# Two graph attention layers in one kernel: the order of chunk 0, the place of layer two's operands, and the order of the mask checks

## The chip, the cores and the metric

One core of a Trainium2 chip. The metric is the device time of one execution in microseconds; the median of several runs is compared.

## What is computed

Two graph attention layers over 4096 nodes with 128 features and a dense 0/1 adjacency matrix `adj` (int32, 4096 x 4096), each followed by a residual and a layer norm:

```python
# layer one, 4 heads of 32
Wh = (h @ W).reshape(N, H, D)
e = leaky_relu(s_src[:, None, :] + s_dst[None, :, :], 0.2)
attention = softmax(where(adj > 0, e, -9e15), axis=1)
x = layernorm(x + elu(einsum('ijh,jhd->ihd', attention, Wh)))
# layer two, hyperbolic maps at the origin
x_tan = logmap0(x)
e = leaky_relu(x_tan @ a[:D] + (x_tan @ a[D:]).T, 0.2)
attention = softmax(where(adj > 0, e, -9e15), axis=1)
x = layernorm(x + proj(expmap0(attention @ x_tan)))
```

## The kernel before

Leaky ReLU has two slopes, so exp(leaky(s_i + d_j)) is a product of a row factor and a column factor on either side of s_i + d_j = 0. The kernel therefore never forms the attention matrix. For each pair it makes two 0/1 masks in fp8 ("above" and "below": edge and sign of the score) and multiplies them on TensorE with column factors times values. These values are kept in three bf16 parts (high, middle, rest) side by side, so that their sum has float32's precision: `moving`, W0 = 198 columns for a head of layer one (2 sides x 3 parts x 33), and 2 x 3 x 129 = 774 columns for a tile of 128 nodes in layer two, 387 for one side.

**Layer one** goes over NC = 4 chunks of 1024 rows. A chunk has U = 32 units: 4 heads times 8 units of JU = 4 column tiles (`u = 8 * head + g`). The masks of a unit are made by ScalarE (`act_unit`, L545, four Sign activations of 1024 elements) or by VectorE (`dve_compare`, L558), as the table `ON_ACT` says, and put together with the edges by VectorE (`dve_unit`: L577 behind ScalarE, L581 behind the comparison, and L587 for the units that need a second mask, by the table `DIRECT`). TensorE then does 64 matmuls (`pe_unit`, L610). `ring` has six slots for units, so ScalarE and VectorE can be up to six units ahead. Behind the second unit of the next head VectorE evacuates a head (`take_head`, L626 to L635); TensorE needs these banks for the next head. The matrix arrives by DMA, is turned on TensorE (`turn_quarter` and `turn_group`) and copied to `masks` by ScalarE (`take_quarter`, L448, and `take_group`, L468). Chunk 0 comes in four quarters, and its values are prepared head by head: `weigh_values` and `take_high` and `take_middle` on VectorE (L480 to L492), `round_part` on ScalarE (L498), in turns. `elu_exp`, `close_piece` and `hidden_sum` close a chunk during the next one.

**Layer two** goes over NR = 8 runs of 512 rows. A run has RT = 4 row tiles and NG = 4 groups of GT = 8 column tiles; 256 matmuls of 387 columns (L969 in runs 0 and 1, group by group; L982 in runs 2 to 7, row tile by row tile). Its masks are kept in DRAM by layer one (`masks_kept`) and loaded per run. ScalarE writes the signs of a group (`signs`, L692, eight activations), VectorE makes both masks of it (`split_group`, L705 and L708). When TensorE has done a row tile of a run, VectorE evacuates it (`evacuate_run`, L716, eight reductions for a run), which frees its two banks for the next run, and then `finish_run` closes the run: L725 to L728, and the closing of L290 to L327 with three activations of ScalarE in between (L336), the last of which is asked for by L322. The operands of layer two are made in four groups of eight tiles: `weigh_group` (L653, L654), `take_high1` (L664), `take_middle1` (L670) on VectorE and `round_part1` (L677) on ScalarE. They need the scores of layer two: roots (L1044), logarithms (L1047) and exponentials (`late_exp`, L763 to L767) on ScalarE between `roots_ask`, `logs_ask`, `gains` and `late_weights` (L1126 to L1131) on VectorE, once for tiles 0 to 23 (EARLY) inside the last chunk, and once for the last eight tiles behind it. Before the change only group 0 is made inside the last chunk.

**Checks.** The kept masks must be 0 or 1. VectorE ORs all of them together in 32 parts (`check_part`, L735), each loaded by GpSimd's queue (L892) in one of three buffers. `raise_flag` looks at the result at the end of run 6.

The order of work is written out by hand: every engine has a loop over c, u (and e in layer two), and `if u == ...` places the extra work behind a unit. Waits are on counting semaphores; an engine works strictly in its program's order. `dve_unit(dve, c, u)` also starts the comparison of unit u + 1, ahead of u's own operations.

## Time and profile before

| | us |
|---|---|
| median of 3 runs | 972.5 (971.72 to 977.3) |
| the profiled execution | 975.74 |
| its span, first to last instruction | 974.0 |
| TensorE busy (matmuls) | 856.1 |
| VectorE busy | 769.9 |
| ScalarE busy | 674.0 |
| GpSimd busy | 43.3 |
| mean granted clock of TensorE | 0.956 |

The profile is of one execution. Its timelines give the start and length of instructions on each engine, the idle time before them and what ended it. Matmuls are pipelined, so the distance between starts is what one costs; the length given for one is longer. "PE" is TensorE's matmuls, "DVE" VectorE, "ACT" ScalarE, "SPq" and "POOLq" the queues from which DMAs are issued. The chunks of layer one end near 183, 305, 428 and 559 us of the span, the runs of layer two lie between 560 and 951.

### The profile page before, as it was taken

How to read it: one execution, taken by the hardware profiler on the slowest of the kernel's cores; microseconds unless marked ns; L12 is line 12 of the kernel's file. 1: busy time of each engine (PE TensorE's matmuls, PEld its weight loads, DVE VectorE, ACT ScalarE, POOL GpSimd, SP SyncE). 2: the span in 40 equal slices, each digit the busy share in tenths (PEclk: the TensorE clock that was granted, in tenths of full speed). 3: DMA queues.
4: the chain of work that ended last, by engine and by line, in shares of the span. 5: the costliest groups of instructions: out<-in, count | busy, mean ns of one | idle time of the engine just before them, and what ended most of it. 6: DMA issues, size and time to landing. Idle time of an engine off the chain costs nothing.

```text
span 974.0 us, 24352 instructions
## 1 busy us (share of the span) xinstructions
PE 856.1 (88%) x10868; PEld 698.2 (72%) x10868; DVE 769.9 (79%) x1312; ACT 674.0 (69%) x789; POOL 43.3 (4%) x80
## 2 busy tenths in 40 slices
PE   8468999989999899999998994899999999879890
PEld 6467999989999899999997952455555555445450
DVE  3857898899988999889976897868565858575865
ACT  3868988888999879999889864873845444426101
POOL 2200000000000000000000000000000010100000
PEclk9879999999999999999999997899999899989995
DMA  8988278704568036040301040202032424241320
GB/s 143 172 83 207 61 72 95 223 23 48 68 75 229 24 38 75 25 196 24 104 9 24 2 152 1 87 23 98 11 109 71 168 81 158 95 159 43 104 87 13
DMA packets 41906, 84.66 MB, mean 87 GB/s; under 512 B 6211, under 2 KB 31173, under 8 KB 41157
## 3 DMA queue, kind: packets, MB, share of 16 engines
q0 software_dynamic: 12416, 33.56, 23.7%
q1 hardware_dynamic: 29380, 49.50, 14.4%
q8 instruction: 86, 1.41, 0.6%
q14 instruction: 24, 0.19, 0.1%
HBM read 112.27 MB, written 21.12 MB: 137 GB/s over the span
## 4 chain that ended last, share of the span: by engine, by line
PE 51%; DVE 27%; ACT 14%; issue 4%; DMA 3%; SPq 0%; DVEq 0%; ACTq 0%
PE bank L610 32%; PE bank L982 9%; ACT masks L692 9%; PE bank L969 6%; DVE ring L558 4%; DVE ring L577 3%; DMA moving<-masks_kept 3%; ACT ring L545 2%; PE bank L461 2%; ACT masks L448 2%; DVE ring L735 1%; DVE ring L587 1%; DVE ring L716 1%; DVE ring L581 1%; ACT moving L498 1%
## 5 line engine op out<-in xcount | busy, mean ns | idle before, releaser
L610 PE MATMUL bank<-moving,ring 128*128 128x99 bf16 (+1 forms) x6400 | 460.5, 220 | 11.6 <-DVE ring L587 7.9
L610 PEld LDWEIGHTS bank<-moving,ring 128*128 128x128 fp8e4 x6400 | 390.3, 98 | 15.3 <-DVE ring L587 8.8
L545 ACT ACTIVATE ring<-s_rows,scores 128x1024 fp8e4<-128x1024 f32 x356 | 377.5, 1142 | 15.6 <-PE bank L610 14.2
L610 PE MATMUL bank<-moving,masks 128*128 128x99 bf16 x1792 | 241.5, 209 | 28.5 <-DVE ring L577 17.2
L610 PEld LDWEIGHTS bank<-moving,masks 128*128 128x128 fp8e4 x1792 | 175.9, 98 | 30.9 <-DVE ring L577 18.1
L982 PE MATMUL bank<-moving,masks 128*128 128x387 bf16 x1152 | 195.9, 328 | 0.0
L982 PEld LDWEIGHTS bank<-moving,masks 128*128 128x128 fp8e4 x1152 | 112.9, 98 | 79.4 <-issue 0.5
L692 ACT ACTIVATE masks<-s_rows,adj_tiles 128x512 fp8e4<-128x512 f32 x256 | 157.8, 709 | 0.1
L336 ACT ACTIVATE ring<-ring 128x4 f32<-128x4 f32 x24 | 4.9, 205 | 190.1 <-DVE ring L292 157.2
L577 DVE SCALAR_TENSOR_TENSOR ring<-ring,masks 128x1024 int32<-128x1024 int32 x89 | 108.4, 1219 | 4.7 <-ACT ring L545 4.7
L587 DVE TENSOR_TENSOR ring<-masks,ring 128x1024 int32<-128x1024 int32 x72 | 88.2, 1225 | 26.3 <-PE bank L610 24.6
L558 DVE TENSOR_SCALAR ring<-s_rows,neg_d 128x1024 uint8<-128x1024 f32 x156 | 107.0, 751 | 0.0
L982 PE MATMUL bank<-adj_tiles,masks 128*128 128x387 bf16 x384 | 73.5, 347 | 20.5 <-DVE ring L716 20.5
L705 DVE SCALAR_TENSOR_TENSOR masks<-masks 128x1024 int32<-128x1024 int32 x32 | 39.2, 1224 | 62.7 <-ACT masks L692 62.6
L969 PE MATMUL bank<-moving,masks 128*128 128x387 bf16 x384 | 65.9, 332 | 20.5 <-DVE masks L708 20.5
L982 PEld LDWEIGHTS bank<-adj_tiles,masks 128*128 128x128 fp8e4 x384 | 39.0, 102 | 51.4 <-DVE ring L716 22.0
L969 PEld LDWEIGHTS bank<-moving,masks 128*128 128x128 fp8e4 x384 | 37.8, 99 | 48.5 <-DVE masks L708 21.7
L468 ACT ACTIVATE masks<-bank 128x1024 uint16<-128x1024 uint16 x48 | 48.5, 1016 | 19.6 <-PE bank L461 18.7
L735 DVE TENSOR_TENSOR ring<-ring,moving 128x1024 int32<-128x1024 int32 x32 | 39.2, 1224 | 19.4 <-DMA moving<-masks_kept 18.2
L581 DVE TENSOR_TENSOR ring<-ring,masks 128x1024 int32<-128x1024 int32 x39 | 47.5, 1218 | 0.0
L626 DVE TENSOR_REDUCE evac<-bank 128x132 f32<-128x396 f32 x64 | 32.8, 562 | 12.7 <-PE bank L610 12.3
L892 POOL DMA_DIRECT2D moving<-masks_kept x32 | 17.0, 531 | 536.3 <-DVE ring L735 353.9
(179 smaller groups left out, 604.5 us busy)
## 6 DMA issues: line engine op xcount, KB each, us to landing
masks_kept<-masks SPq DMA_DIRECT2D x4, 4096.0 KB, 18.3
masks<-masks_kept SPq DMA_DIRECT2D x8, 2048.0 KB, 12.0
moving<-masks_kept POOLq DMA_DIRECT2D x32, 512.0 KB, 5.0
adj_tiles<-in_adj_dram POOLq DMA_DIRECT2D x24, 512.0 KB, 8.3
s_rows<-score_rows SPq DMA_DIRECT2D x14, 512.0 KB, 5.8
adj_tiles<-in_adj_dram POOLq DMA_DIRECT2D x16, 256.0 KB, 15.3
feat<-in_x_dram SPq DMA_DIRECT2D x4, 512.0 KB, 5.7
values_kept<-masks SPq DMA_DIRECT2D x1, 2048.0 KB, 14.3
```

Of the source, the lines that this page charges most:

```text
L468: act.activation(dst[:, j:j + GQ, t * P:(t + 1) * P], turn_bank[q % 4][:, :].bitcast(U16).rearrange("p (j i) -> p j i", i=P), ACT.Copy, bi ...
L545: last = act.activation(j_tile(below, k), s_rows[:, h % 2, :], ACT.Sign, bias=scores[:, g * JU + k, h:h + 1], saturate=False)
L558: last = dve.tensor_scalar(j_tile(below, k), s_rows[:, h % 2, :], neg_d[:, h, j:j + 1], float(TWO), ALU.is_lt, ALU.mult)
L577: dve.scalar_tensor_tensor(out=below, in0=below, scalar=1, in1=m, op0=ALU.logical_shift_right, op1=ALU.bitwise_and).then_inc(done, 1)
L581: dve.tensor_tensor(below, below, m, ALU.bitwise_and).then_inc(done, 1)
L587: dve.tensor_tensor(above_slot(c, u).bitcast(I32), m, below, ALU.bitwise_xor).then_inc(unit_ready, 1)
L610: last = pe.matmul(bank[b][:, at + lo:at + hi], mask, moving[:, j, h, lo:hi], start=first, stop=(j == T - 1), skip_group_check=True)
L692: last = act.activation(j_tile1(sides_of_run[y][1], j), s_rows1[:, y, :], ACT.Sign, bias=d1[:, j:j + 1], saturate=False)
L705: dve.scalar_tensor_tensor(out=mine, in0=mine, scalar=1, in1=here, op0=ALU.logical_shift_right, op1=ALU.bitwise_and).then_inc(below1_ready, 1)
L735: dve.tensor_tensor(seen, seen, check_in[k % CB], ALU.bitwise_or).then_inc(check_done, 1)
L969: last = pe.matmul(bank[2 * t + side][:, 0:PARTS * K1], j_tile1(sides_of_run[e][side], j)[:, t * P:(t + 1) * P], moving1(g)[:, j % GT, sid ...
L982: last = pe.matmul(bank[2 * t + side][:, 0:PARTS * K1], j_tile1(sides_of_run[e % 2][side], j)[:, t * P:(t + 1) * P], moving1(j // GT)[:, j ...
```

## The change

- **Checks.** The 32 ORs were done in rows of six or seven behind the splits of runs e + 2, from e = 2 on. Now there is one behind each `split_group` of the runs e + 2 with e > 0, one before and one behind `finish_run` for e = 2 to 6, and what is left before `raise_flag`. The three buffers move out of `moving` (to the free end of `ring`, `first_part` and `second_part`), and the first load also waits for `factors_asked` 2.
- **Chunk 0, head 0.** VectorE compares unit u + 1 behind the operations of unit u. `weigh_values`, `take_high` and `take_middle` of heads 1 to 3 stand behind other units, so do `round_part`, `take_quarter(2)` and the turning of the last quarter.
- **Layer two's operands.** Group 1 (tiles 8 to 15) is prepared inside the last chunk. For it and group 2 the columns are those of heads 0 and 1, and of 2 and 3, of tiles 0 to 23 of `moving`: a column tile's side lies in three pieces of 129, one in each of three tiles, H * W0 = 792 elements of bf16 apart. Group 3 has tiles 24 to 31 of `moving` for itself. The early roots, logarithms, exponentials and group 0 move three units forward.
- **Behind the last chunk** groups 2 and 3, the closing of the chunk and the late scores are in another order on VectorE and ScalarE.

```diff
+        late_operands = late[:, 0:2 * GT * W1].bitcast(BF16).rearrange("p (t w) -> p t w", w=W1)
+        last_operands = moving[:, PARTS * GT:T, :, :].rearrange("p t h w -> p t (h w)")
+
+        def operand1(g, k, side):
+            if g == 0:
+                return late_operands[:, k, side * PARTS * K1:(side + 1) * PARTS * K1]
+            if g == NG - 1:
+                return last_operands[:, k, side * PARTS * K1:(side + 1) * PARTS * K1]
+            return moving[:, PARTS * k:PARTS * (k + 1), 2 * (g - 1) + side, 0:K1]
+
...
-        free = (NG - 1) * GT * W1
-        check_in = [moving_flat[:, free + n * 2 * CHECK:free + (n + 1) * 2 * CHECK].bitcast(I32) for n in range(3)]
+        check_in = [of_ring(CHECK).bitcast(I32), first_part[:, 0:CHECK].bitcast(I32), second_part[:, 0:CHECK].bitcast(I32)]
...
-            if g + 1 < UH and not ON_ACT[c * U + u + 1]:
+            compare_next = g + 1 < UH and not ON_ACT[c * U + u + 1]
+            if compare_next and (c > 0 or h > 0):
                 dve_compare(dve, c, u + 1)
             below = below_slot(c, u).bitcast(I32)
...
+            if compare_next and c == 0 and h == 0:
+                dve_compare(dve, c, u + 1)
...
         def weigh_group(dve, g):
-            sides = early_sides if g == 0 else late_sides
+            sides = early_sides if g < 2 else late_sides
             js = slice(g * GT, (g + 1) * GT)
             for b in range(2):
-                if g > 1:
+                if g % 2 == 1:
                     dve.wait_ge(moving1_ready, 2 * g)
                 dve.tensor_tensor(sides[b][:, :, 0:F], feat[:, js, :], over((above_w1, below_w1)[b][:, js], GT, F), ALU.mult)
                 dve.tensor_copy(sides[b][:, :, F:K1], (above_d1, below_d1)[b][:, js].rearrange("p (t o) -> p t o", o=1))\
                     .then_inc(cast1_asked, 1)
 
-        def moving_part(g, b, q):
-            return moving1(g)[:, :, (b * PARTS + q) * K1:(b * PARTS + q + 1) * K1]
...
                     if k == 0:
                         pool.wait_ge(kept, 16 * NC)
+                        pool.wait_ge(factors_asked, 2)
...
-                        if c == 0 and u in (0, 2, 4):
-                            turn_quarter(pe, u // 2 + 1)
+                        if c == 0 and u in (0, 2, 5):
+                            turn_quarter(pe, {0: 1, 2: 2, 5: 3}[u])
...
-                                                         moving1(g)[:, j % GT, side * PARTS * K1:(side + 1) * PARTS * K1],
+                                                         three(operand1(g, j % GT, side)),
...
                         if c == 0:
-                            if u in (1, 3, 5):
-                                round_part(act, u // 2 + 1, 0)
-                            if u in (2, 4, 6):
-                                round_part(act, u // 2, 1)
-                            if u == 2:
+                            if u in (2, 3, 4):
+                                round_part(act, u - 1, 0)
+                                round_part(act, u - 1, 1)
+                            if u == 3:
                                 act.wait_ge(scores_out, 16)
                                 take_quarter(act, 2)
                             if u == 4:
...
                         if c > 0 and u == 4:
                             elu_exp(act, c - 1)
                         if c == NC - 1:
-                            if u == 18:
+                            if u == 15:
                                 act.wait_ge(roots_asked, 1)
                                 act.activation(rows[:, 2:4, 0:EARLY], rows[:, 0:2, 0:EARLY], ACT.Sqrt).then_inc(roots_given, 1)
-                            if u == 20:
+                            if u == 17:
                                 act.wait_ge(logs_asked, 1)
                                 act.activation(rows[:, 8:10, 0:EARLY], rows[:, 8:10, 0:EARLY], ACT.Ln).then_inc(logs_given, 1)
+                            if u == 20:
+                                late_exp(act, 0)
                             if u == 23:
-                                late_exp(act, 0)
-                            if u == 27:
                                 round_part1(act, 0, 0)
-                            if u == 29:
+                            if u == 25:
                                 round_part1(act, 0, 1)
+                            if u == 28:
+                                round_part1(act, 1, 0)
+                            if u == 30:
+                                round_part1(act, 1, 1)
                 signs(act, 0, 0)
-                act.wait_ge(moving1_ready, 2)
+                act.wait_ge(moving1_ready, 4)
                 signs(act, 0, 1)
-                round_part1(act, 1, 0)
-                round_part1(act, 1, 1)
                 elu_exp(act, NC - 1)
-                signs(act, 0, 2)
-                round_part1(act, 2, 0)
-                round_part1(act, 2, 1)
                 act.wait_ge(roots_asked, 2)
                 act.activation(rows[:, 2:4, EARLY:T], rows[:, 0:2, EARLY:T], ACT.Sqrt).then_inc(roots_given, 1)
+                round_part1(act, 2, 0)
                 act.wait_ge(logs_asked, 2)
                 act.activation(rows[:, 8:10, EARLY:T], rows[:, 8:10, EARLY:T], ACT.Ln).then_inc(logs_given, 1)
+                round_part1(act, 2, 1)
+                signs(act, 0, 2)
                 late_exp(act, 1)
+                signs(act, 0, 3)
                 round_part1(act, 3, 0)
-                signs(act, 0, 3)
                 round_part1(act, 3, 1)
                 for g in range(NG):
...
                         if c == 0:
-                            if u in (0, 2, 4):
+                            if u == 0:
+                                weigh_values(dve, 1)
+                            if u == 1:
+                                take_high(dve, 1)
+                            if u == 2:
+                                take_middle(dve, 1)
+                            if u in (3, 5):
                                 weigh_values(dve, u // 2 + 1)
                                 take_high(dve, u // 2 + 1)
-                            if u in (1, 3, 5):
                                 take_middle(dve, u // 2 + 1)
                         else:
                             if u == TAKE_AT:
...
                             if u in PIECES_AT[:5]:
                                 close_piece(c - 1, PIECES_AT.index(u))
                         if c == NC - 1:
-                            if u == 15:
+                            if u == 12:
                                 roots_ask(step, rows, 0, EARLY, roots_asked)
-                            if u == 17:
+                            if u == 14:
                                 dve.wait_ge(roots_given, 1)
                                 logs_ask(step, rows, inv_std, 0, EARLY, logs_asked)
-                            if u == 19:
+                            if u == 16:
                                 dve.wait_ge(logs_given, 1)
                                 gains(step, rows, inv_std, 0, EARLY, d1, s1, scores1_ready)
-                            if u == 22:
+                            if u == 19:
                                 late_weights(0)
-                            if u == 23:
+                            if u == 20:
                                 dve.wait_ge(kept, 16 * (NC - 1))
                                 dve.wait_ge(unit_done, (NC - 1) * U)
                                 weigh_group(dve, 0)
-                            if u == 26:
+                            if u == 22:
                                 take_high1(dve, 0)
-                            if u == 29:
+                            if u == 24:
                                 take_middle1(dve, 0)
+                            if u == 25:
+                                dve.wait_ge(unit_done, (NC - 1) * U + 2 * UH)
+                                weigh_group(dve, 1)
+                            if u == 27:
+                                take_high1(dve, 1)
+                            if u == 30:
+                                take_middle1(dve, 1)
                 split_group(dve, 0, 0)
                 take_head(step, NC - 1, H - 1)
-                dve.wait_ge(unit_done, NC * U)
-                weigh_group(dve, 1)
-                take_high1(dve, 1)
-                take_middle1(dve, 1)
                 split_group(dve, 0, 1)
-                close_piece(NC - 1, 0)
-                weigh_group(dve, 2)
-                take_high1(dve, 2)
-                take_middle1(dve, 2)
-                split_group(dve, 0, 2)
-                for n in range(1, 5):
+                for n in range(3):
                     close_piece(NC - 1, n)
                 step.need(summed_at[0])
                 roots_ask(step, rows, EARLY, T, roots_asked)
+                dve.wait_ge(unit_done, NC * U)
+                weigh_group(dve, 2)
+                close_piece(NC - 1, 3)
                 dve.wait_ge(roots_given, 2)
                 logs_ask(step, rows, inv_std, EARLY, T, logs_asked)
+                take_high1(dve, 2)
+                close_piece(NC - 1, 4)
+                take_middle1(dve, 2)
+                step.need(summed_at[0])
                 dve.wait_ge(logs_given, 2)
                 gains(step, rows, inv_std, EARLY, T, d1, s1, scores1_ready)
                 late_weights(1)
                 weigh_group(dve, 3)
+                split_group(dve, 0, 2)
                 take_high1(dve, 3)
                 take_middle1(dve, 3)
                 split_group(dve, 0, 3)
...
                     if e == 0:
                         for g in range(2, NG):
                             split_group(dve, 1, g)
+                    if 2 <= e < NR - 1:
+                        check_part(dve, done)
+                        done += 1
                     finish_run(step, e)
+                    if 2 <= e < NR - 1:
+                        check_part(dve, done)
+                        done += 1
                     if e + 2 < NR:
                         for g in range(NG):
                             split_group(dve, e + 2, g)
+                            if e > 0:
+                                check_part(dve, done)
+                                done += 1
                     if e == 0:
                         begin_checks(dve)
-                    while done < CHECKS * max(e - 1, 0) // (NR - 3) and done < CHECKS:
-                        check_part(dve, done)
-                        done += 1
                     if e == NR - 2:
...
```

## Rows read from the trace of the kernel before

**Rows 1.** busy time by stretch: run 2 alone, then run 5 with the gap after it
```profile
667.90:710.50 42.60, 42.60 (x258) 25.04 (x256) 27.74 (x66) 22.79 (x37) 0.00 (x0) 1.00 0.19 62
848.10:906.40 58.30, 44.47 (x257) 25.51 (x257) 38.80 (x75) 22.79 (x37) 5.31 (x10) 0.91 0.39 134
```

**Rows 2.** timeline of PE (start, us, instructions, idle before): starts of runs 4 to 7
```profile
756.96 5.35 PE L982 MATMUL bank<-adj_tiles,masks 128*128 128x387 bf16 x16 [3.83 <-DVE ring L716]
...
805.27 2.84 PE L982 MATMUL bank<-adj_tiles,masks 128*128 128x387 bf16 x16 [2.78 <-DVE ring L716]
858.17 4.51 PE L982 MATMUL bank<-adj_tiles,masks 128*128 128x387 bf16 x16 [10.11 <-DVE ring L716]
906.39 4.30 PE L982 MATMUL bank<-adj_tiles,masks 128*128 128x387 bf16 x16 [3.77 <-DVE ring L716]
...
942.49 8.15 PE L982 MATMUL bank<-moving,masks 128*128 128x387 bf16 x48
```

**Rows 3.** timeline of DVE around the end of run 3
```profile
745.58 3.88 DVE L735 TENSOR_TENSOR ring<-ring,moving 128x1024 int32<-128x1024 int32 x3
...
755.88 3.82 DVE L716 TENSOR_REDUCE ring<-bank 128x129 f32<-128x387 f32 x8
...
771.26 0.17 DVE L322 TENSOR_SCALAR ring<-ring 128x4 f32<-128x4 f32 x1
...
776.70 1.22 DVE L705 SCALAR_TENSOR_TENSOR masks<-masks 128x1024 int32<-128x1024 int32 x1 [2.65 <-ACT masks L692]
...
792.56 1.22 DVE L708 TENSOR_TENSOR masks<-masks 128x1024 int32<-128x1024 int32 x1
```

**Rows 4.** timeline of PE from the start of run 0 to run 1
```profile
560.17 10.83 PE L969 MATMUL bank<-adj_tiles,masks 128*128 128x387 bf16 x64 [0.67 <-DVE evac L626]
...
613.17 12.13 PE L969 MATMUL bank<-moving,masks 128*128 128x387 bf16 x64 [19.02 <-DVE masks L708]
625.14 10.81 PE L969 MATMUL bank<-adj_tiles,masks 128*128 128x387 bf16 x64
```

**Rows 5.** timeline of DVE between the last chunk and group 3 of run 0
```profile
561.66 1.22 DVE L653 TENSOR_TENSOR ring<-feat,adj_tiles 128x1024 f32<-128x1024 f32 x1
...
568.83 1.22 DVE L705 SCALAR_TENSOR_TENSOR masks<-masks 128x1024 int32<-128x1024 int32 x1
...
608.34 2.38 DVE L670 TENSOR_TENSOR moving<-ring,moving 128x1032 bf16<-128x1032 f32 x2 [4.61 <-ACT moving L677]
```

**Rows 6.** timeline of ACT in the last chunk, and the signs of run 5
```profile
498.65 0.24 ACT L1047 ACTIVATE adj_tiles<-adj_tiles 128x48 f32<-128x48 f32 x1 [3.27 <-DVE adj_tiles L362]
...
513.88 16.73 ACT L545 ACTIVATE ring<-s_rows,scores 128x1024 fp8e4<-128x1024 f32 x16
...
536.80 2.22 ACT L677 ACTIVATE adj_tiles<-masks 128x1032 bf16<-128x1032 f32 x2
...
547.45 9.92 ACT L692 ACTIVATE masks<-s_rows,adj_tiles 128x512 fp8e4<-128x512 f32 x16
...
771.57 19.70 ACT L692 ACTIVATE masks<-s_rows,adj_tiles 128x512 fp8e4<-128x512 f32 x32
```

**Rows 7.** timeline of DVE in the last chunk: what it waits for
```profile
522.33 1.23 DVE L577 SCALAR_TENSOR_TENSOR ring<-ring,masks 128x1024 int32<-128x1024 int32 x1 [2.47 <-ACT ring L545]
528.82 0.57 DVE L626 TENSOR_REDUCE evac<-bank 128x132 f32<-128x396 f32 x1 [5.26 <-PE bank L610]
```

**Rows 8.** the checks' loads: list of waits of runs 2 to 7; DMA issues
```profile
DVE ring L735 <- DMA moving<-masks_kept: 18.2, 15, 3.5
...
moving<-masks_kept POOLq DMA_DIRECT2D x32, 512.0 KB, 5.0
```

**Rows 9.** timeline of DVE and of ACT in chunk 0
```profile
64.89 1.26 DVE L487 TENSOR_TENSOR first_part<-first_part,moving 128x1056 f32<-128x1056 f32 x1 [9.36 <-ACT moving L498]
...
98.31 1.99 DVE L626 TENSOR_REDUCE evac<-bank 128x132 f32<-128x396 f32 x4
...
91.73 20.92 ACT L545 ACTIVATE ring<-s_rows,scores 128x1024 fp8e4<-128x1024 f32 x20 [0.19 <-ACT ring L545]
```

27 lines of the change are left out of this document (17 added, 10 removed).

## The prediction

> **What bounds it now.** I read the busy time by stretches of 50 us first. TensorE carries the middle of every chunk of layer one (48 to 50 us busy of 50), and loses time at chunk starts, where VectorE is late, in the first 100 us, and in layer two (36.8 to 46 of 50). Then I read the list of waits and the timelines of PE, DVE and ACT there.
>
> Layer two, runs 2 to 7. Run 2 takes 42.60 us with PE busy all of it: 256 matmuls at 166 ns [rows 1]. That is the floor of a run. From run 4 on each run starts with PE idle, 3.83, 2.78, 10.11 and 3.77 us, released by L716, the evacuation of the run before, and three of the starts are followed by 16 matmuls that take 4.3 to 5.35 us instead of 2.84, at a lower granted clock (0.91 over the stretch of run 5 and its gap) [rows 1, 2]. L716 is late because VectorE still does the checks' ORs (L735, six or seven in a row behind the four splits, in which it also waits for their loads), and only then evacuates: after run 3, which PE ended at 753.1, it began at 755.88, with eight reductions in 3.82 us [rows 3]. Meanwhile, during the four splits, it waited 2.65 us and about 2.4 us three times more for ScalarE's signs [rows 3].
>
> Between the layers. Groups 0, 1 and 2 of run 0 start fairly close to one another, then PE waits 19.02 us for group 3; the 64 matmuls behind take 12.13 instead of 10.8 us [rows 4]. VectorE works almost through from 561.66 until PE gets group 3 at 613.17 [rows 4, 5]: three operand groups, three splits, the last chunk's closing, the scalars. Its one large wait is 4.61 us, for a rounding which stands on ScalarE behind eight signs [rows 5].
>
> The last chunk. All three engines are nearly full. ScalarE computes units without a pause from 513.88 on, and VectorE waits 2.47 us for it, then 5.26 us for PE at the head's end [rows 6, 7].
>
> **The change, term by term** (against the profiled execution's span, 974.0 us).
>
> *Spread ORs.* Take 0 as the moment when PE ends a run. Tile 3 is evacuated at +1.0. One OR, 1.25 (3.88 for three), makes it +2.3. From the end of the evacuation, 759.70, to L322, which asks for the last root, is 11.7, and ScalarE starts the signs right behind it, 11.87 after the evacuation [rows 3, 6]: +14.2. The second OR falls into the 2.65 us that VectorE waits for the first signs. Four groups of signs in 19.70 [rows 6]: +33.9. Three of the four ORs behind splits fall into waits of about 2.4 us; the last split (2.45) and the fourth OR end at +37.6. Evacuation of tiles 0 to 2 of the next run: +38.6 for the first, +40.5 for the third. PE needs tile 0's bank at +42.6, so it has 4.0 us of slack, and the cycle is PE's: 42.6. Each load has at least two spacings of some 5 us before it is wanted, because three buffers are kept, against 5.0 us from issue to landing [rows 8]. So from the start of run 2 (667.9) to the end of run 7 (942.49 + 8.15 = 950.6) 282.7 becomes 6 x 42.6 = 255.6: **-27.1**. This includes the slow matmuls behind the gaps. The ORs left over at the end of run 6, two, precede the flag while PE computes run 7 and cost nothing; without that cover 2.5 us.
>
> *Chunk 0.* Comparing unit u+1 after unit u, and roundings in another order on ScalarE, take away VectorE's 9.36 us wait [rows 9], and unit 1 is ready some 9 us sooner. But group 3 is then weighed only after unit 5, and quarter 3's copies stand behind its roundings, so the gap moves to units 4 and 6. Adding up the same durations in the new order, ScalarE ends unit 8 at 94.7 instead of 95.9 (it runs without pause from 91.73), and the first evacuation starts at 97.1 instead of 98.31 [rows 9]: **-1.2**. The bounds are -4 and +1. PE is full behind it, so it lasts.
>
> *Last chunk.* This is where I expect a loss. The exponentials of the early scores move on ScalarE from unit 23 to 20, and their partner on VectorE (late_weights) from 22 to 19. The offset is the same, but ScalarE runs ahead: it stands before unit 21 at 494, where it waited 3.27 us for the logarithms until 498.65 [rows 6]. VectorE reaches the end of unit 19 no earlier than 504.5, because the root and gain chains (4.6 and 1.7 us) now go in front of head 1's evacuation, which ends at 498.0; units 18 and 19 with the comparison of unit 20 (2.74) take 6.3, and late_weights' first two operations 0.2. ScalarE is idle for about 10 us, and the units queued behind it start with unit 21 at 504.9: +6.1. The exponentials, which took 2.4 us ahead of the unit at 513.88, are then done already: -2.4. The roundings of group 1, two pairs at 2.2 (536.80) [rows 6], are added: +4.4. It ends unit 31 at 555.6 and not 547.4. A unit costs it 4.2 (16.73 for four). On VectorE take_middle of group 0, now at unit 24, waits for a rounding that ScalarE does behind unit 25, and head 2's evacuation comes at 532.5 instead of 528.82 [rows 7]. PE's last unit ends at 563.0 instead of 559.5. And split_group(0, 0) stands before the last head's evacuation and waits for eight signs, 4.96 us (9.92 for 16), behind unit 31, until 560.7 [rows 6]. The evacuation ends at 565.2, and run 0 starts there instead of 560.17 [rows 4]: **+5.0**. Bounds: 0, if VectorE's added 7.2 us and ScalarE's 4.4 fit in the 7.7 us of waits [rows 7], and 8.
>
> *Between the layers.* Group 1's preparation is gone from here: 561.66 to 568.83, 7.2 us. The wait of 4.61 goes too, as roundings alternate with scalars; I count 2.3 of new waits (0.7 at the exponentials, 1.3 at group 3's first rounding). VectorE's 51.4 us become 51.4 - 7.2 - 5.0 + 2.3 = 41.5 [rows 5], with its small waits counted in the 5.0. But the order puts the scalars ahead of group 2's split, which ends 33 us after the last head is taken: 567.0 + 33 = 600.0. Groups 0 and 1 keep PE until 586.8. Now PE is idle 13 us before group 2 and not 19 before group 3. Group 2 takes 12.1 at the low clock (as group 3 did), group 3 follows at 612.1 (its split is done at 608.5), and run 1 starts at 622.9 instead of 625.14 [rows 4]: -7.2 against the later start, **-2.2** with the +5.0 in it. Run 1's signs are ready 4.9 us after one another from 609.6, in time.
>
> *Strided operands.* Groups 1 and 2 are read as three pieces of 129 columns, 1584 bytes apart. No matmul of before reads so. Bounds: 0, and 10 ns for two more breaks, as a matmul of 387 columns takes 166.4 ns where its columns at 2.4 GHz are 161.3, so about 5 ns per start: 896 matmuls in runs 1 to 7 by 10 = 9 us. I take 0, the columns in a piece being contiguous as before.
>
> *Adding the pool's wait for factors_asked* costs nothing: the loads it holds back aren't needed before run 1's end.
>
> Sum: -27.1 - 1.2 - 2.2 = -30.5. From 974.0 that is 943.5. The median of the runs shown is 972.5, 1.5 below the span (and 3.2 below that execution's own 975.74), and the same step from it gives **942.0**.
>
> **Rivals.**
> 1. *The last chunk hides the added work* (0.15). For it: VectorE waits 7.7 us there. Against: ScalarE has no such reserve. 942 - 5 = 937.
> 2. *The strided operand costs per piece* (0.10): 942 + 9 = 951. The Trainium skill's "SBUF — State Buffer", section "Door 1: The DMA port swizzle", says that reads run at full bandwidth inside a 16-byte line and pay at each new line; three pieces touch a few lines more than one, it gives no price, and no row here shows one. By that rule this rival holds.
> 3. *The loads are late for the spread ORs* (0.12). Now VectorE waits up to 3.5 us for one, 18.2 us in 15 waits [rows 8]. If both ORs that nothing covers, the first and the last of a run, wait so, 37.6 + 7 makes tile 0 free at +45.6: 3 us over the floor in four or five runs, 942 + 13 = 955. Against: the buffers are refilled 10 us and more ahead.
> 4. *Slower:* the strided operand reads at a lower rate. The mechanism is in the 896 matmuls that are on the path; it decides from 30.5 us / 896 = 34 ns each, a fifth of 166. At half rate it would be 942 + 896 x 0.166 = 1091. The transposes and weight loads of before read with steps, but no moving operand does; 0.03.
> 5. *The spreading does little*, because another wait, the masks or scores of a run behind ScalarE's start at +14, takes the ORs' place and runs stay near 47 us: 942 + 25 = 967. Now the signs start 18 us after a run's end, so these loads were never tested at 14. 0.04.
>
> **How the numbers follow.** The forecast has 0.56. The bounds of chunk 0 and of the last chunk (-8 to +5) and the two positive cases of 9 and 13 us make the range 932 to 956, which leaves out rivals 4 and 5 and a little on either side. What a measurement of this kernel can tell from no change is about 1%, 9.7 us: faster 0.93 (forecast, rivals 1 to 3), same 0.04 (5), slower 0.03 (4).
>
> **What would show it.** Right: runs 2 to 7 each 42.6 us with PE busy and clock 1.00; L735 one at a time between L708 and L705; a single PE gap of 11 to 15 us, before group 2 of run 0; ScalarE idle some 10 us before L766 around 500; run 0 starting near 564 to 565. Wrong: PE gaps at run starts that L716 still ends; matmuls with `moving` above 170 ns apart in groups 1 and 2 only; L735 waiting for DMA; ScalarE never idle around 500 (rival 1).

## The result, and the profile after

The changed kernel took **941.4 us** (median, 940.55 to 943.84) where the kernel before took 973.1 beside it. The ratio is 0.9675 (0.9643 to 0.9706), so it is 31.7 us faster. A second measurement of the same pair gave 941.64 against 974.58, a ratio of 0.9663 (0.9645 to 0.9681). The span of the profiled execution is 942.1 us.

**Layer two, runs 2 to 7.** The page's costliest groups (busy time, mean ns of one, idle before it), first from before, then the line that answers to it after:

```profile
L982 PE MATMUL bank<-adj_tiles,masks 128*128 128x387 bf16 x384 | 73.5, 347 | 20.5 <-DVE ring L716 20.5
```
```profile
L999 PE MATMUL bank<-adj_tiles,masks 128*128 128x387 bf16 x384 | 67.8, 328 | 0.0
```

The 20.5 us of idle time ahead of a run's first matmul are gone. The busy time by stretch of runs 2 and 5 of the changed kernel answers to [rows 1]: no idle time, clock 1.00, and 42.43 us where it was 42.60.

```profile
664.15:706.58 42.43, 42.43 (x258) 24.78 (x257) 32.39 (x70) 22.79 (x37) 2.12 (x4) 1.00 0.36 112
791.44:833.87 42.43, 42.43 (x258) 24.78 (x257) 33.01 (x68) 22.79 (x37) 3.17 (x6) 1.00 0.43 137
```

The timeline of DVE after run 3, whose end is at 749.0, answers to [rows 3]. The ORs (L751; L735 in the kernel before) stand one at a time, at +1.1, +16.5, +21.6 and so on, the last at +36.2, and the evacuation of tiles 0 to 2 (L732) follows at +37.4. ScalarE's signs (second fence) start at +14.1.

```profile
750.12 1.21 DVE L751 TENSOR_TENSOR ring<-ring,first_part 128x1024 int32<-128x1024 int32 x1
...
765.46 1.22 DVE L751 TENSOR_TENSOR ring<-ring,second_part 128x1024 int32<-128x1024 int32 x1
...
770.61 1.22 DVE L751 TENSOR_TENSOR ring<-ring 128x1024 int32<-128x1024 int32 x1
...
785.21 1.22 DVE L751 TENSOR_TENSOR ring<-ring 128x1024 int32<-128x1024 int32 x1
786.35 2.89 DVE L732 TENSOR_REDUCE ring<-bank 128x129 f32<-128x387 f32 x6
```
```profile
763.08 19.70 ACT L708 ACTIVATE masks<-s_rows,adj_tiles 128x512 fp8e4<-128x512 f32 x32
```

**Between the layers.** The timeline of PE from run 0 to run 1 answers to [rows 4]. Run 0 starts 4.0 us later, the wait stands before group 2 and is 12.99 us instead of 19.02, and run 1 starts 3.4 us earlier.

```profile
564.16 10.83 PE L986 MATMUL bank<-adj_tiles,masks 128*128 128x387 bf16 x64 [0.67 <-DVE evac L645]
574.83 10.77 PE L986 MATMUL bank<-moving,masks 128*128 128x387 bf16 x64
598.60 23.30 PE L986 MATMUL bank<-moving,masks 128*128 128x387 bf16 x128 [12.99 <-DVE masks L724]
621.73 3.49 PE L986 MATMUL bank<-adj_tiles,masks 128*128 128x387 bf16 x20
```

**The last chunk.** ScalarE waits 9.93 us for late_weights' first operations (first fence, which answers to [rows 6]), and VectorE waits twice for roundings that ScalarE has not got to (second fence, which answers to [rows 7]).

```profile
504.60 0.23 ACT L782 ACTIVATE adj_tiles<-adj_tiles 128x24 f32<-128x24 f32 x1 [9.93 <-DVE adj_tiles L1145]
...
554.53 5.63 ACT L708 ACTIVATE masks<-s_rows,adj_tiles 128x512 fp8e4<-128x512 f32 x9
```
```profile
518.64 2.38 DVE L680 TENSOR_TENSOR masks<-masks,adj_tiles 128x1032 f32<-128x1032 f32 x2 [4.12 <-ACT adj_tiles L693]
528.86 2.38 DVE L686 TENSOR_TENSOR adj_tiles<-masks,adj_tiles 128x1032 bf16<-128x1032 f32 x2 [3.82 <-ACT adj_tiles L693]
532.29 1.99 DVE L645 TENSOR_REDUCE evac<-bank 128x132 f32<-128x396 f32 x4
```

**Chunk 0.** The unit behind the first head starts at 97.41 instead of 99.02, but chunk 3 starts at 434.60 and before at 434.36. By this one pair of traces nothing was left of the gain. The experiments take that up.

### The profile page after: what moved, and what is told of

It reads as the page before. It is cut to its first block, busy times and chain, and to the rows that moved or that the text cites. A ratio compares the mean times of both kernels' runs of the same rounds, so it can differ in the third digit from the quotient of the medians.

```text
span 942.1 us, 24354 instructions
## 1 busy us (share of the span) xinstructions
PE 851.5 (90%) x10868; PEld 699.0 (74%) x10868; DVE 766.5 (81%) x1312; ACT 674.1 (72%) x789; POOL 43.2 (5%) x80
## 4 chain that ended last, share of the span: by engine, by line
PE 63%; DVE 21%; ACT 11%; issue 4%; DMA 0%; SPq 0%; DVEq 0%; ACTq 0%
PE bank L999 27%; PE bank L629 25%; PE bank L986 7%; ACT ring L561 6%; DVE ring L574 4%; DVE ring L594 4%; PE bank L477 2%; DVE ring L604 2%; ACT masks L464 2%; DVE ring L598 1%; DVE evac L645 1%; ACT masks L708 1%; PE bank L937 1%; ACT moving L514 1%; DVE stats L414 1%
## 5 line engine op out<-in xcount | busy, mean ns | idle before, releaser
L629 PE MATMUL bank<-moving,masks 128*128 128x99 bf16 x1792 | 246.1, 211 | 24.3 <-DVE ring L594 12.5
L629 PEld LDWEIGHTS bank<-moving,masks 128*128 128x128 fp8e4 x1792 | 178.2, 100 | 26.1 <-DVE ring L594 17.7
L999 PE MATMUL bank<-adj_tiles,masks 128*128 128x387 bf16 x384 | 67.8, 328 | 0.0
L999 PEld LDWEIGHTS bank<-adj_tiles,masks 128*128 128x128 fp8e4 x384 | 37.6, 98 | 26.3
L732 DVE TENSOR_REDUCE ring<-bank 128x129 f32<-128x387 f32 x64 | 31.5, 551 | 26.3 <-PE bank L999 22.5
L598 DVE TENSOR_TENSOR ring<-ring,masks 128x1024 int32<-128x1024 int32 x39 | 47.5, 1218 | 0.1
L724 DVE TENSOR_TENSOR masks<-masks 128x1024 int32<-128x1024 int32 x32 | 39.2, 1225 | 1.1
```

Source lines behind the costliest of these rows:

```text
L598: dve.tensor_tensor(below, below, m, ALU.bitwise_and).then_inc(done, 1)
L629: last = pe.matmul(bank[b][:, at + lo:at + hi], mask, moving[:, j, h, lo:hi], start=first, stop=(j == T - 1), skip_group_check=True)
L999: last = pe.matmul(bank[2 * t + side][:, 0:PARTS * K1].rearrange("p (q k) -> p q k", q=PARTS), j_tile1(sides_of_run[e % 2][side], j)[:, t ...
```

## The experiments

### One part at a time

**a_chunk0_only** is the kernel before with the new order of chunk 0 only:

```diff
-                            if u in (0, 2, 4):
-                                weigh_values(dve, u // 2 + 1)
-                                take_high(dve, u // 2 + 1)
-                            if u in (1, 3, 5):
-                                take_middle(dve, u // 2 + 1)
+                            if u == 0:
+                                weigh_values(dve, 1)
...
+                            if u in (3, 5):
+                                weigh_values(dve, u // 2 + 1)
+                                take_high(dve, u // 2 + 1)
+                                take_middle(dve, u // 2 + 1)
```

> The kernel before with the new order of chunk 0 and nothing else. The prediction: 1.2 us faster, and the gain lasts to the end. The rival, read from the two traces: unit 8 starts 1.6 us sooner and the shift is there until about 223 us, then PE's granted clock falls for a few us at the start of chunk 1's last head and the shift is gone, so 0 +- 0.5 us in all. A trace in which the clock stays at 1.00 between 215 and 235 us and the shift lasts would say that the loss was an accident of one execution.

Measured: 970.43 us against 972.95, ratio 0.9969 (0.9956 to 0.9983), so about 2.5 to 3 us faster, where the prediction's term was 1.2. Its profiled execution is the slowest of its eleven (973.01 us): the clock was 0.92 and 0.74 in the two halves of 220 to 230 us, and chunk 3 started at 435.01, so by this trace alone the rival would hold.

**b_spread_only** is the kernel before with the ORs spread only (the last hunk of the diff).

> The kernel before with the 32 ORs spread as in the change, buffers where they were. The prediction's term: 27.1 us faster, 945 to 946 us, runs 2 to 7 back to back at 42.6 us. The rival that another wait (masks or scores of a run, or the ORs' loads) takes the place of the ORs: less than 20 us, PE gaps at the run starts still. If the pieces of the operands decide the matmuls' pace, here 48 matmuls out of moving still take 8.15 us and not 8.10.

Measured: 949.22 us, ratio 0.9752 (0.9732 to 0.9772), 23.7 us faster, where the term was 27.1. No run from 2 to 7 has a gap at its start.

**c_operands_only** is the changed kernel with chunk 0's order and the ORs as before, so it has the last chunk, the place between the layers and the three-piece operand alone.

> The change without the new order of chunk 0 and with the ORs in rows behind the splits as before: only the operands' part (group 1 in the last chunk, the three pieces, the order behind the last chunk, the buffers). The prediction: 5.0 lost in the last chunk, 7.2 gained behind it, 2.2 us faster than before; the traces of the two kernels say 3.4 to 3.6 with the loss 3.8 to 4.0. Rival, that the gain comes from somewhere else (its parts only pay with the spread ORs, which would have hidden run 1's earlier end): 0.

Measured: 968.99 us, ratio 0.9968 (0.9953 to 0.9983), about 3 to 4 us faster. PE's gaps at run starts are back (4.14, 4.19, 5.25 and 4.12 us), the one before group 2 is 12.99 us, run 0 starts at 563.09. The prediction's terms for this part are 2.2 us together.

The three differences add up to 30.2 us (2.5 + 23.7 + 4.0), and the whole change measured 31.7 and 32.9. Each is known to about 1.5 to 2 us, so the parts add up, and nothing large comes from their meeting.

The same three kernels settle the matmul with the strided operand. The timelines of PE show the last 48 matmuls that read `moving`, in b with the old layout (one piece of 387 columns) and in the changed kernel with three pieces of 129:

```profile
916.04 8.15 PE L982 MATMUL bank<-moving,masks 128*128 128x387 bf16 x48
```
```profile
910.69 8.10 PE L999 MATMUL bank<-moving,masks 128*128 128x387 bf16 x48
```

From the start of these 48 to the next matmul that reads `adj_tiles` are, at the other row tiles of a run, 7.99 us (166.4 ns each) and 7.94 (165.4). Only 32 of the 48 read three pieces: taken by group, from a group's first start to the next group's, it is 165.8 ns for group 1 and 165.0 for group 2, where b has 166.4 for both. Group 3 lies in one piece in either kernel and went from 166.6 to 165.5 too. So the three pieces cost nothing, and the 1 ns by which the matmuls are faster is not shown to come from them. A run is 42.43 instead of 42.6 us. The matmuls that read `adj_tiles` take 2.82 and 2.83 us for 16 in either kernel.

### What ScalarE's wait costs

**d_factors_early** is the changed kernel with the two operations that ScalarE waits for moved from late_weights(0) to right behind the gains, three units earlier on VectorE:

```diff
                                 gains(step, rows, inv_std, 0, EARLY, d1, s1, scores1_ready)
+                                ask_factors(0)
...
-                    dve.tensor_scalar(rows[:, 0, lo:hi], s1[:, lo:hi], 0.0, None, ALU.min)
-                    dve.tensor_scalar(rows[:, 1, lo:hi], s1[:, lo:hi], 0.0, None, ALU.max).then_inc(factors_asked, 1)
```

> The change with one move: the two operations of VectorE that ScalarE's second pair of exponentials waits for stand right behind the gains at unit 16 and not at unit 19. If ScalarE's idle 9.9 us before L782 is what makes the last chunk 4 us longer, that wait goes, head 3 starts 4 us sooner (529 instead of 533 us), run 0 at 560, and the kernel takes 937 us, 4 us less than the change. If the last chunk is longer because of the added work alone (VectorE's 7.2 us, ScalarE's 4.4), under 1 us.

Measured: **935.78 us** (934.21 to 937.24), ratio 0.9615 (0.9593 to 0.9636). That is 5.6 us less than the changed kernel, more than the wait at head 3 alone, 4.4, would give. From chunk 3's start to run 2's start it is 223.3 us in d and 229.6 in the changed kernel. Of these 6.3 us, 5.7 are there when run 0 starts: it starts 129.6 us after chunk 3 in the changed kernel and 123.8 in d. ScalarE's chain makes the whole of that. Its signs for run 0 stand behind its units of the last chunk, and VectorE's split of them stands ahead of the last head's evacuation, for which run 0 waits. The signs begin at 554.53 in the changed kernel, 119.9 us after chunk 3's start, and 114.2 us after it in d (timeline of ACT):

```profile
548.19 9.92 ACT L708 ACTIVATE masks<-s_rows,adj_tiles 128x512 fp8e4<-128x512 f32 x16
```

PE's wait ahead of head 3 shrinks with it, from 4.69 to 0.30 us. The timelines of PE, changed kernel and d:

```profile
533.00 0.24 PE L629 MATMUL bank<-moving,masks 128*128 128x99 bf16 x1 [4.69 <-DVE evac L645]
```
```profile
528.19 0.20 PE L629 MATMUL bank<-moving,masks 128*128 128x99 bf16 x1 [0.30 <-PE bank L629]
```

The busy time by stretch shows that in the changed kernel the granted clock (the figure behind the busy times) also falls, in and behind that wait, and in d stays at 1.00:

```profile
525.00:535.00 10.00, 5.31 (x87) 0.80 0.00 0
535.00:545.00 10.00, 10.00 (x146) 0.86 0.01 2
```
```profile
525.00:535.00 10.00, 9.70 (x169) 9.57 (x167) 8.61 (x15) 9.01 (x10) 0.00 (x0) 1.00 0.01 2
535.00:545.00 10.00, 10.00 (x187) 9.97 (x186) 9.96 (x11) 10.00 (x11) 0.00 (x0) 1.00 0.01 2
```

From head 3's start to run 0's are 31.2 us in the changed kernel and 29.6 in d, and it would be easy to put these 1.6 us down to the clock. They are not the clock's. In j, the changed kernel measured again (below), PE's wait ahead of head 3 was 1.26 us and the clock stayed at 1.00 in the same stretches, yet from head 3's start (530.03) to run 0's (561.16) are 31.1 us there too:

```profile
525.00:535.00 10.00, 8.74 (x155) 8.62 (x153) 8.97 (x14) 10.00 (x10) 0.00 (x0) 1.00 0.01 3
535.00:545.00 10.00, 9.74 (x171) 9.59 (x169) 9.93 (x13) 10.00 (x11) 0.00 (x0) 1.00 0.01 2
```
```profile
561.16 5.16 PE L986 MATMUL bank<-adj_tiles,masks 128*128 128x387 bf16 x30 [1.94 <-DVE evac L645]
```

In all six traces with this order of the last chunk (the changed kernel, j, c, e, f and m) run 0 starts 129.5 to 129.6 us after chunk 3, at a clock of 0.74 to 1.00 from 525 to 535. The slow matmuls only made PE's wait ahead of run 0 shorter, 0.67 us in the changed kernel where j has 1.94.

**g_factors_and_takes** is d with take_high1(0) and take_middle1(0) one unit later:

```diff
-                            if u == 22:
+                            if u == 23:
                                 take_high1(dve, 0)
-                            if u == 24:
+                            if u == 25:
                                 take_middle1(dve, 0)
```

> The kernel with the factors' two operations moved up (d_factors_early, 935.8 us), and besides it take_high1(0) and take_middle1(0) of VectorE moved one unit back, from units 22 and 24 to 23 and 25. Theory: in d TensorE has no gap over 0.3 us at head 3 of the last chunk and bounds that stretch, so nothing is left for VectorE to give: within 0.5 us of d, 935.3 to 936.3, and head 3 starts at 528.2 again. Rival: VectorE's two waits for ScalarE's rounding at 518.64 and 528.86 in the changed kernel (4.12 and 3.82 us) still hold TensorE in d, and go with the move: about 2 us less than d, 934.

Measured: 936.63 us (936.31 to 939.07), ratio 0.9634 (0.9616 to 0.9653). That is 0.85 above d, just outside what was expected, and the intervals of the two do not separate them; the rival's gain of 2 us is not there. The traces are further apart than the times: from chunk 3's start to run 2's are 226.1 us in g, 2.9 more than in d. The timeline of DVE shows that it stands idle at the head's end, waiting for PE, and the take that could have been done in that wait comes behind the evacuation, at 526.85.

```profile
522.54 0.57 DVE L645 TENSOR_REDUCE evac<-bank 128x132 f32<-128x396 f32 x1 [3.34 <-PE bank L629]
...
526.85 2.37 DVE L686 TENSOR_TENSOR adj_tiles<-masks,adj_tiles 128x1032 bf16<-128x1032 f32 x2
```

PE then waits for VectorE three times in head 3, 0.85, 0.73 and 0.38 us. ScalarE waits 2.51 us, 0.86 in d, for weigh_group(1), which now stands behind take_middle1(0) (timeline of ACT):

```profile
530.67 2.29 ACT L693 ACTIVATE moving<-masks 128x1032 bf16<-128x1032 f32 x2 [2.51 <-DVE masks L673]
```

Its signs begin 116.6 us after chunk 3's start and not 114.2, and run 0 starts 126.2 us after it and not 123.8: 2.4 of the 2.9 us, by the same chain as above. The time is nearer to d's than that because this execution lost nothing to the clock in the chunks before (chunk 3 starts at 430.89, 433.97 in d).

**k_group2_first** is d with another order between the layers: group 2 is weighed, taken and split before the last closings and the gains, group 3 behind them, ScalarE's roundings and signs to match.

```diff
                 take_head(step, NC - 1, H - 1)
+                dve.wait_ge(unit_done, NC * U)
+                weigh_group(dve, 2)
                 split_group(dve, 0, 1)
-                for n in range(3):
-                    close_piece(NC - 1, n)
+                take_high1(dve, 2)
+                close_piece(NC - 1, 0)
+                take_middle1(dve, 2)
+                close_piece(NC - 1, 1)
+                split_group(dve, 0, 2)
+                close_piece(NC - 1, 2)
```

> d_factors_early with another order on VectorE and ScalarE between the layers: group 2 of layer two is prepared and split for run 0 before the last five pieces of the evacuation are closed, group 3 after them. Theory: the 13.0 us in which TensorE waits ahead of group 2 (at 592.2 in d) are the closing and the gains, which only group 3 must wait for. With group 2 ready first TensorE has its 10.6 us of work while these run: no gap ahead of group 2, about 11 us ahead of group 3, run 1 about 2.4 us earlier than in d, 933.4 us in all. Rival: the work is only put in another order and the same sum stands ahead of the last group: run 1 starts where it did, 935.8.

Measured: **934.98 us** (934.39 to 936.03), ratio 0.9610 (0.9594 to 0.9626). It has the lowest median of all, but only 0.8 us below d, and the two intervals do not separate them. The gap went where it was expected, ahead of group 3:

```profile
600.87 4.38 PE L986 MATMUL bank<-moving,masks 128*128 128x387 bf16 x15 [11.72 <-DVE masks L724]
```

It shrank from 13.00 to 11.72 only, 1.3 us, and from chunk 3's start to run 2's is 1.0 us less than in d (222.3 against 223.3). The rival that the same sum stands ahead of the last group is nearer than the 2.4 us expected.

### How much slack VectorE has in a run

**e_two_more** and **f_six_more** are the changed kernel with two and six more ORs of a check's size, on padding, ahead of finish_run in runs 2 to 6. They do this work on top of the computation.

```diff
                         check_part(dve, done)
                         done += 1
+                        for _ in range(6):
+                            step(dve.tensor_tensor(padding, padding, padding, ALU.bitwise_or))
                     finish_run(step, e)
```

> The changed kernel with two more ORs of check's size (1.25 us each, one behind the other, on padding) ahead of finish_run in each of runs 2 to 6: 5 x 2.5 = 12.5 us more of VectorE. Theory: in the changed kernel VectorE is 4.0 us ahead at the first tile of a run, so TensorE doesn't see it: within 1 us of 941.4. Rival: VectorE is already the bound there and the work adds in full: 953.9.

> The same with six more ORs: 7.5 us more of VectorE in each of runs 2 to 6, 37.5 in all. Theory: the slack of 4.0 us is used up. The first such run is late by 3.6 us, and from then VectorE's own round of work (about 40.4 + 7.5 = 47.9 us against TensorE's 42.4) sets the pace: 3.6 + 3 to 4 x 5.5, about 20 us more, 961 (955 to 964). Rival: each run starts again at TensorE's pace and loses all 7.5: 941.4 + 37.5 = 978.9. Other rival: the slack holds all of it, 941.4.

Measured: e 940.44 us (940.21 to 940.84), f 963.75 (961.21 to 963.88). The two were measured side by side: 12.5 us more of VectorE's work cost nothing, and f is 23 us above e and 22 above the changed kernel, with 20 expected. The timeline of PE in f:

```profile
751.96 4.50 PE L1000 MATMUL bank<-adj_tiles,masks 128*128 128x387 bf16 x16 [3.44 <-DVE ring L733]
799.48 4.49 PE L1000 MATMUL bank<-adj_tiles,masks 128*128 128x387 bf16 x16 [3.28 <-DVE ring L733]
847.00 4.49 PE L1000 MATMUL bank<-adj_tiles,masks 128*128 128x387 bf16 x16 [3.28 <-DVE ring L733]
894.54 4.41 PE L1000 MATMUL bank<-adj_tiles,masks 128*128 128x387 bf16 x16 [3.29 <-DVE ring L733]
```

The first gap is 3.44 us, so 7.5 us of work came out 3.44 late: the slack of a run is 4.06 us. From then on runs are 47.5 us apart. Behind each gap 16 matmuls take 4.5 us instead of 2.83, 1.7 us more, and 3.3 + 1.7 are 5.0 of the 5.1 us by which a run is longer. That does not make the slow matmuls a price of each run: between 752 and 900 us VectorE never waits for PE in this trace, so its own round of 47.5 us sets the pace, and at full clock the gap would be 1.7 us longer instead. Only behind the last gap do they add. By this trace the six ORs cost 3.4 + 3 x 5.1 + 1.7 = 20.4 us. Work up to the slack of 4 us costs nothing; beyond it each us costs itself, and 1.7 us more once.

### Chunk 0, once more

The trace of the changed kernel said that chunk 0's gain is gone by chunk 3, the time of a said that it is not. So the pair was run again, beside **m_no_chunk0**, the changed kernel with chunk 0's old order (the edit of a, reversed).

> The kernel before, unchanged. Its time again (972 to 974), and which clock its profiled execution is granted at 210 to 215, at 220 to 230 and at 345 to 350 us. In the profiled executions so far the old order of chunk 0 (before, b_spread_only, c_operands_only) had clock 1.00 from 220 to 230 each time, and below 0.8 at 345 to 350 in two of three. Theory: the same again, unit 24 of chunk 0 (start at 224.3) to the next half chunk in 58.5 us. Rival: the place of the lower clock is chance in either kernel, and then it stands at 220 to 230 here as often as there.

> The changed kernel, unchanged: 941.4 within 1.5 us. Of eight profiled executions that hold the new order of chunk 0 (after, a, d, e, f, g, h, k) six had a granted clock of 0.72 to 0.94 in both slices of 220 to 230 us, and lost 1.6 us in them; e and g had 1.00 there, kept chunk 0's 1.5 us, and e's first 664 us are the same instructions as those of the changed kernel. Theory: the lower clock there is the answer to the new order, likely but not in each execution; 6 in 8 that it is seen here too.

> The changed kernel with chunk 0's old order (the take_high and take_middle of VectorE, the rounding of ScalarE, the compare and the quarter as before). Theory: chunk 0's new order gives 1.5 us at unit 8 and loses 1.6 of them again in six of eight executions to the lower clock at 220 to 230: 0.3 us on average, so this kernel is 0 to 0.7 us above j_after_again. Rival, the prediction's term: the gain lasts, 1.2 to 1.6 us above. Other rival: a_chunk0_only's 3.0 us are chunk 0's own, 3 us above.

(The start at 224 us that the first of these calls unit 24 of chunk 0, and a's expectation chunk 1's last head, is that of the second head of chunk 1.)

Measured: i 973.76 us (971.32 to 978.91), j 941.64 (941.09 to 942.90), m **944.07** (943.10 to 944.52). No time of m is as low as the highest of j. Chunk 0's order is worth 2.4 us, not 0 to 0.7.

The busy time by stretch tells what the first pair of traces hid. The changed kernel, and then e, whose first 664 us are the same instructions:

```profile
220.00:225.00 5.00, 3.17 (x43) 0.88 0.48 39
225.00:230.00 5.00, 5.00 (x64) 0.78 0.65 69
```
```profile
220.00:225.00 5.00, 3.17 (x51) 2.90 (x48) 4.91 (x8) 3.89 (x4) 0.53 (x1) 1.00 0.48 38
225.00:230.00 5.00, 5.00 (x81) 5.00 (x78) 4.92 (x8) 4.15 (x5) 0.00 (x0) 1.00 0.66 70
```

64 matmuls against 81 in the same 5 us. From the start at 222.8 to the one two heads on it is 60.12 us in the changed kernel (222.89 to 283.01) and 58.51 in e (222.75 to 281.26): 1.6 us lost to the clock. The same stretch one chunk later, from 345 us on, does it too. Over all profiled executions:

| | new order (9 executions) | old order (5) |
|---|---|---|
| start at 224 us, mean | 222.37 | 224.61 |
| clock below 1.00 at 205 to 215 us | 2 of 9 | 4 of 5 |
| clock below 1.00 at 220 to 230 us | 7 of 9 | 0 of 5 |
| clock below 1.00 at 345 to 350 us | 6 of 9 | 4 of 5 |
| start of chunk 3, mean (lowest to highest) | 433.2 (430.9 to 435.0) | 434.4 (433.5 to 435.4) |

So the new order gains 2.2 us up to 224 us, most executions give 1.6 of them back at 220 to 230, and 1.2 us are left on average at chunk 3. The places of the lower clock vary between executions of identical instructions, so one execution's chunk 3 start says nothing within 2 us. The expectations for i and j held: i had 1.00 there, j 0.71 and 0.95. The new order does not bring the lower clock on, it moves it: between 205 and 230 us 4 of 5 executions of the old order have it too, but ahead of 215 us, as here in the kernel before:

```profile
210.00:215.00 5.00, 5.00 (x82) 0.69 0.29 108
```

There it costs nothing. From the start of the first head of chunk 1 to that of the second are 35.1 us in before, i, b and m, which have it, and in c (189 to 225 us in each), which has not, since PE waits for VectorE in that stretch (1.2 to 2.2 us at a time) and slow matmuls only shorten these waits. Behind the second head's start PE is busy without a break (5.00 of 5.00 us above), and there it costs 1.6. Which difference of the new order moves it stays open, and so does why m's difference of 2.4 us is twice the 1.2 of the means; five times of each kernel are few.

The Trainium skill, page "TensorE: Matmul & The Clock Gate", section "What's actually happening", says that how many matmuls of the same kernel run at the slow level at its start varies from run to run. The traces show the same in mid-kernel: 58.5 or 60.1 us for the same instructions.

### Stalls for which no wait is shown

In every trace PE loses some time in the last chunk with the mark "issue", in which it waits for nothing that is shown. Before, six such stalls of 0.18 to 1.23 us fall between 515.8 and 525.1, 3.2 us together (the expectation below says 5.5). After, 2.61 and 0.18 fall between 505 and 508.4. Both lie behind one transfer, the 12 KB store of the early scores in 4-byte pieces, on SP's queue. Here are that store and a stall, for before, and for the changed kernel:

```profile
508.80 0.38 SPq L744 DMA_DIRECT2D score_rows<-adj_tiles  x1
...
525.04 0.20 PE L610 MATMUL bank<-moving,masks 128*128 128x99 bf16 x1 [1.23 <-issue]
```
```profile
493.57 0.38 SPq L760 DMA_DIRECT2D score_rows<-adj_tiles  x1
...
508.32 1.72 PE L629 MATMUL bank<-moving,ring 128*128 128x99 bf16 x28 [2.61 <-issue]
```

**h_store_late** is d with that store held back:

```diff
                 load_masks(sp, 0)
+                sp.wait_ge(unit_done, (NC - 1) * U + 24)
                 late_scores(sp, 0)
```

> d_factors_early with one wait more on SyncE: the 12 KB store score_rows<-adj_tiles of the last chunk in 4-byte pieces, issued at about 493 us in the changed kernel, goes only when unit 24 of the chunk is done, at about 531. Theory: TensorE's stalls in the last chunk for which the trace shows no wait (3.0 us at 505 to 508 in the changed kernel, 5.5 us at 515 to 525 in the kernel before, each 7 to 16 us behind that store) come with the store: here none at 505 to 508, and 2 to 5 us of them between 538 and 548; head 3 starts 2 to 3 us earlier than in d (about 525.7), run 0 within 1.5 us of d's 557.8, and the whole within 1.5 us of d. Rival: the stalls belong to a place in the instructions (TensorE's own, or ScalarE's) and stay at 505 to 508 though the store is gone.

Measured: 939.26 us (938.35 to 941.68). The timelines of SP and of PE:

```profile
524.65 0.38 SPq L760 DMA_DIRECT2D score_rows<-adj_tiles  x1
```
```profile
533.11 0.20 PE L629 MATMUL bank<-moving,masks 128*128 128x99 bf16 x1 [1.18 <-issue]
...
535.28 0.24 PE L629 MATMUL bank<-moving,ring 128*128 128x198 bf16 x1 [0.73 <-issue]
...
537.90 0.32 PE L629 MATMUL bank<-moving,ring 128*128 128x198 bf16 x1 [1.99 <-issue]
```

No stall is left at 505 to 508, head 3 starts at 524.92 (3.3 us earlier than in d), and 3.9 us of stalls stand 7.3 to 13.3 us behind the store's new time. They moved with the store and did not stay with an instruction. In all 14 traces they stand 7 to 16.3 us behind it. In the five traces that show its landing (a, c, d, h and the changed kernel), 15.1 to 16.6 us behind its issue, they end before that. What this transfer takes away from PE the trace doesn't show, nor was the store tried in larger pieces. That the small pieces matter is not shown either: a stall with the same mark, of 0.4 to 1.8 us, stands at 307 to 310 us in 13 of the 14 traces (not in d), 9 to 10 us behind the issue of a chunk's 4 MB store of masks.

The place was a bad one. The store was issued at 524.65 and not 531, so the stalls came before the 538 to 548 expected. And from head 3's start to the end of PE's last unit are 34.2 us against 28.2 in d: 3.9 of stalls, and by estimate 1.7 at a clock of 0.83 over the 10 us from 535 to 545. Here PE is what run 0 waits for, and it starts at 559.82, 2.0 us behind d. The time is 3.5 us above d, where 1.5 at most were expected, for run 0 and for the whole.

## Why the prediction was right, point by point

The forecast was 942.0 and 941.4 and 941.6 were measured.

**Spread ORs, -27.1.** The mechanism was right in each step that the traces show. Forecast and trace, in us after a run's end: signs +14.2 and +14.1, end of the signs +33.9 and +33.8, end of the last OR +37.6 and +37.4, slack 4.0 and, by f, 4.06. The floor of 42.6 was 42.43. The size was off by 2.5: with b's 255.8 us for runs 2 to 7 the term is measured against 280.4, the mean of three executions with the ORs as before (i, a and c), and that is **-24.6**; in time b gave 23.7. The step that failed is that it took one execution's 282.7. Its gap of 10.11 us [rows 2] was out of the ordinary: at the same place i, a and c have 4.44, 4.76 and 5.25. The timeline of PE in i, the same kernel again, and its list of waits for that stretch, against 3.5 us for the longest in [rows 8]:

```profile
755.39 4.36 PE L982 MATMUL bank<-adj_tiles,masks 128*128 128x387 bf16 x16 [3.90 <-DVE ring L716]
...
803.71 5.36 PE L982 MATMUL bank<-adj_tiles,masks 128*128 128x387 bf16 x16 [4.02 <-DVE ring L716]
...
853.85 4.49 PE L982 MATMUL bank<-adj_tiles,masks 128*128 128x387 bf16 x16 [4.44 <-DVE ring L716]
...
901.98 4.44 PE L982 MATMUL bank<-adj_tiles,masks 128*128 128x387 bf16 x16 [3.69 <-DVE ring L716]
```
```profile
DVE ring L735 <- DMA moving<-masks_kept: 16.0, 13, 1.6
```

The gaps are 16.1 us there, and 17.1 and 17.7 in a and c, where the profile before had 20.5. That profile's execution was 3.2 us above its median. The prediction saw this and took its terms off the median in full nevertheless, though part of what made that execution long was in the term.

**Chunk 0, -1.2.** PE's gaps moved to units 4 and 6 (6.44 and 6.10 us), as said. The gain at the first head's end is 1.6 us in the first pair of traces and 2.2 in the means at 224 us. "PE is full behind it, so it lasts" was wrong in its reason: a lower clock behind 220 us takes 1.6 back in most executions. What lasted is 1.2 us by the means of the traces and 2.4 by m against j; the forecast's bounds held both.

**Last chunk, +5.0.** ScalarE's idle time was 9.93 us where about 10 was forecast, its start again 504.60 where 504.5, head 2's evacuation 532.29 where 532.5, PE's last unit ended at 563.5 where 563.0, the signs of run 0 began at 554.5 where 555.6. Run 0 started 4.0 us later and not 5.0; the missing 1.0 is that of the signs, which began 1.1 us earlier than forecast. What the steps left out, the stalls of the store (2.8 us, 3.2 before) and the clock behind the 4.69 us gap, did not set run 0's start: it is the same in the six traces with 2.6 to 3.8 us of stalls and with or without the lower clock. In the order of before PE is the bound there, and the stalls count in full: run 0 starts 123.3, 123.9, 124.6 and 125.8 us after chunk 3 in a, i, b and before, with 0.9, 1.3, 2.1 and 3.2 us of them. Taken over more traces the term was as large as forecast: the mean of those four is 124.4, and the six with the new order have 129.5 to 129.6, 5.1 more. d shows that this was not the price of the added work: with two operations of 0.17 us moved, run 0 starts 123.8 us after chunk 3, no later than before the change. Rival 1 (the last chunk hides the work) was right about what is possible, and wrong about this order.

**Between the layers, run 1 2.2 earlier.** It was 3.4, with a gap of 12.99 us before group 2 where 13 was forecast. Of the 1.2 difference 1.0 is the last chunk's. By the means of the traces named above, from run 0's start to run 2's is 8.2 us less, where 7.2 was forecast, and with the 5.1 lost ahead of it 3.1 us are gained. c puts the whole part, with the 0.17 us per run from the matmuls, at 3 to 4 us in time.

**Strided operands, 0.** Right. Rival 2 falls, with the figures of b and the changed kernel above. The Trainium skill's rule on 16-byte lines ("SBUF — State Buffer", "Door 1: The DMA port swizzle") would give the added pieces a price; none is seen with pieces of 258 bytes whose starts are 1584 bytes apart (165.0 and 165.8 ns against 166.4), and the measurement decides.

**Rivals 3 to 5.** In the changed kernel's list of waits of runs 2 to 7 no OR waits for a DMA, so the loads are in time; the operand does not read at a lower rate; and no other wait took the ORs' place, since e shows room for two more.

The sum, then: -24.6, -1.2 to -2.4 and -3 to -4 are 29 to 31 us where 30.5 was forecast and 31.7 and 32.9 were measured. That the forecast came out within 0.6 us is partly luck: the first term was 2.5 too large and the other two together 1 to 3 too small.

## What to carry to other kernels

Before a term is taken from a gap, look at whether its repeats agree; a 10.11 beside 2.78, 3.83 and 3.77 was for the most part one execution's accident (4.4 to 5.3 in three others) and not a saving, and a profiled execution above the median holds such accidents. When work is moved ahead on one engine, ask what the other engine waits for in it: here two operations of 0.17 us at the wrong place cost 5.6 us, and moving them apart from the work that they came with gave a version faster than either kernel. A clock that falls is not a cost by itself: where PE waits for another engine anyway, as at 210 us and ahead of run 0 here, the slow matmuls only shorten the wait. Look at what ends the next wait, and at a second execution with another clock, before its loss is added up. A short filler behind a long chain is free up to the slack, which could be counted here from durations to 0.1 us.

## What the runs showed of the hardware that was not expected

- Behind one 12 KB store in 4-byte pieces, 15 to 17 us under way, TensorE has 0.7 to 3.9 us of stalls with no wait shown, 7 to 16.3 us behind its issue, at either of the places tried. The same mark stands behind a 4 MB store too (0.4 to 1.8 us), so the pieces are not shown to be the reason.
- The same instructions are granted another clock from one execution to the next: 1.6 us more or less in each of two stretches in which PE is the bound, up to 3.3 us at the start of chunk 3 (e against the changed kernel), and nothing where it waits for VectorE anyway (129.5 to 129.6 us from chunk 3 to run 0 at clocks of 0.74 to 1.00).
- A moving operand in three pieces of 129 columns is no slower than one of 387: 165.0 and 165.8 ns against 166.4.
